# Self-attention in a decoder kernel: ScalarE copies the second bank of transposed probabilities in every step, VectorE the first bank only

## The reference, cut to what matters

```python
b, s, d = x.shape                      # s = 128 tokens in the kernel's view: (16, 128, 128)
xn = _rmsnorm(x, gamma1)
q, k, v = ...                          # 16 heads of 64
q, k = _rope(q, theta), _rope(k, theta)
scores = jnp.where(causal, jnp.einsum('bhqd,bhkd->bhqk', q, k) * scale, -jnp.inf)
attn = jax.nn.softmax(scores, axis=-1)
ctx = jnp.einsum('bhqk,bhkd->bhqd', attn, v)
attn_out = ctx @ o_w + o_b + xn
an = _rmsnorm(attn_out, gamma2)
aff = jax.nn.softmax(an @ router_w + router_b, axis=-1)
topv, topi = jax.lax.top_k(aff, K_ACT) # 3 of 31 experts per token
```

## Time and profile before

| | before |
|---|---|
| time, median of 3 executions | 1320.45 us (1319.38 to 1323.55) |
| the profiled execution: its own time | 1318.47 us |
| its span in the profile | 1316.7 us |
| PE busy | 1040.7 us, 79% of the span |
| DVE busy | 793.7 us, 60% |
| ACT busy | 579.6 us, 44% |
| POOL busy | 343.4 us, 26% |
| groups 0, 1, 2 of self-attention | from about 679 to 925 us, some 82 us each |
| group 3 with its `finish` pieces | from about 925 to 1059 us |
| experts | from about 1059 us to the end |

### The profile page before, as it was taken

The page is one execution under the profiler, slowest core; times in us unless marked ns, Lnnn a source line. Parts: engine busy times, 40 slices in busy tenths (PEclk is TensorE's granted clock), DMA queues, the critical chain, the costliest instruction groups (busy, mean ns, idle before and its releaser), DMA issues.

```text
span 1316.7 us, 20312 instructions
## 1 busy us (share of the span) xinstructions
PE 1040.7 (79%) x6091; PEld 660.4 (50%) x6121; DVE 793.7 (60%) x2206; ACT 579.6 (44%) x1439; POOL 343.4 (26%) x374
## 2 busy tenths in 40 slices
PE   5395575674768988988479989899876699999994
PEld 2242341331445665655136665666544566666662
DVE  6727638438455777676357667576665256666565
ACT  5345345345335777766124354343533133333331
POOL 3320320221351011111246456464742200000001
PEclk9597697786877999999579999999987689999997
DMA  5000000000000000000022212122110000000001
GB/s 170 2 17 6 2 16 6 2 16 0 0 12 29 13 25 14 1 1 1 14 60 56 65 38 58 40 56 64 33 41 1 1 13 16 20 16 19 17 16 37
DMA packets 43287, 33.37 MB, mean 25 GB/s; under 512 B 11266, under 2 KB 34018, under 8 KB 43234
## 3 DMA queue, kind: packets, MB, share of 16 engines
q1 hardware_dynamic: 43234, 32.70, 9.5%
HBM read 14.85 MB, written 1.05 MB: 12 GB/s over the span
## 4 chain that ended last, share of the span: by engine, by line
PE 61%; issue 18%; DVE 11%; POOL 6%; ACT 4%; SPq 0%; POOLq 0%; DMA 0%; DVEq 0%; ACTq 0%
PE psum L1675 10%; PE psum L1667 8%; PE psum L1542 5%; PE psum L1631 4%; PE psum L1595 4%; PE psum L1363 3%; PE psum L1370 3%; PE psum L1486 3%; PE psum L1611 3%; PE psum L1549 2%; PE psum L1556 2%; PE psum L1473 2%; PE psum L1467 2%; DVE negmax L1061 2%; POOL rT L568 2%
## 5 line engine op out<-in xcount | busy, mean ns | idle before, releaser
L1264 DVE SCALAR_TENSOR_TENSOR ntok<-psum,gate,ntok 128x128 f32<-128x128 f32 x512 | 144.3, 344 | 95.0 <-PE psum L1675 88.3
L1675 PEld LDWEIGHTS psum<-we,area 128*128 128x128 f32 x1024 | 129.2, 191 | 59.2 <-issue 30.8
L893 ACT ACTIVATE area<-psum,b1s 128x512 f32<-128x512 f32 x128 | 88.0, 687 | 150.3 <-PE psum L1667 147.7
L1675 PE MATMUL psum<-we,area 128*128 128x128 f32 x1024 | 137.9, 281 | 0.0
L865 ACT ACTIVATE area<-psum,negmax 128x128 f32<-128x128 f32 (+1 forms) x256 | 104.0, 423 | 69.1 <-DVE negmax L1165 69.1
L666 POOL TENSOR_TENSOR area<-area,rinv 128x512 f32<-128x512 f32 x64 | 94.3, 1474 | 140.3 <-DVE rinv L1221 140.3
L1667 PE MATMUL psum<-area,we 128*128 128x512 f32 x256 | 127.2, 600 | 0.0
L1128 DVE SCALAR_TENSOR_TENSOR area<-psum,ccol,cs 128x512 f32<-128x512 f32 x128 | 90.0, 745 | 52.4 <-PE psum L1542 51.0
L1542 PE MATMUL psum<-area,qkw 128*128 (+1 forms) x128 | 79.0, 702 | 35.4 <-DVE area L1134 18.4
L1061 DVE TENSOR_REDUCE negmax<-psum 128x2 f32<-128x512 f32 x128 | 82.3, 685 | 40.1 <-PE psum L1473 40.0
L797 ACT ACTIVATE area<-psum,negmax 128x256 f32<-128x256 f32 x256 | 102.0, 510 | 3.0 <-DVE negmax L1061 3.0
(11 more groups left out here) (215 smaller groups left out, 2002.2 us busy)
## 6 DMA issues: line engine op xcount, KB each, us to landing
area<-area SPq DMA_DIRECT2D x256, 64.0 KB, 2.0
we<-in_L_ffn_re_w SPq DMA_DIRECT2D x62, 64.0 KB, 1.8
area<-in_L_attn_W SPq DMA_DIRECT2D x8, 256.0 KB, 3.0
area<-in_mask_BxSxS_ik SPq DMA_DIRECT2D x8, 256.0 KB, 2.8
area<-in_x SPq DMA_DIRECT2D x4, 256.0 KB, 3.5
area<-in_ctx SPq DMA_DIRECT2D x8, 128.0 KB, 2.2
out<-ntok SPq DMA_DIRECT2D x4, 256.0 KB, 2.3
qkw<-in_L_ffn_q_w SPq DMA_DIRECT2D x1, 512.0 KB
```

The lines of the kernel that those rows point to most:

```text
L1264: last = nc.vector.scalar_tensor_tensor(res[:, n, :], bank[2 + g % 2][:, i * D:(i + 1) * D], gate[:, n, bass.ds(e, 1)], res[:, n, :], ALU. ...
L1675: last = nc.tensor.matmul(bank[2 + g % 2][:, i * D:(i + 1) * D], hE[:, g % 2, i * 128:(i + 1) * 128], we2[:, slot, :], start=True, stop=True)
```

## The change

In groups 0 to 3 the copy of bank 5 in the even steps goes from DVE to ACT. One constant changes; two places read it, which stay as they are.

```diff
         PARTS = ((0, 0, 1, 1), (0, 1, 0, 1))
-        ACT_COPIES = (1, 3)
+        ACT_COPIES = (0, 1, 2, 3)
         SU = 16
```

## The result

| | before | changed |
|---|---|---|
| time, median (6 runs each, taken together) | 1320.52 us (1318.38 to 1323.55) | 1328.37 us (1327.74 to 1329.41) |
| ratio, 95% interval | | 1.006 (1.0047 to 1.0073) |
| the profiled execution: time, span | 1318.47, 1316.7 us | 1327.88, 1326.1 us |

The forecast was 1322.2 us, the range ended at 1326.7. The kernel became slower by 7.9 us, outside both. First the page of the changed kernel: its span, its busy times, and the clock row of 40 slices.

The account below looks back on a forecast made before the run. PE was taken as nearly full in the loop (74.22 of 82.00 us). The terms 0 + 0.50 + 0.50 + 0.75 = +1.75 us on the median 1320.45 made 1322.2 us; the range was 1318.3 to 1326.7.

Parts of the forecast that it names:

- Bound and loop: Groups 0 to 2: PE nearly full, removed DVE time falls into its waits; 0, range -0.4 us per pass to nothing.
- Step 2 of the loop: Tightest place in groups 0 to 2: ACT's copy ends 1.76 us before PE's second half of turn(1) needs it.
- Step 4: Group 3: PE waits 0.46 us for ACT's copy; later POOL holds DVE's L1179 and L1187; +0.50 us.
- the bound without the lock: Group 3, step 4: cost if POOL did not hold DVE through shared SBUF ports, +0.05 us.
- Step 8: Group 3: ACT's queue 0.50 us later up to DVE's maxima; PE's scores delay caught in idle time; +0.50 us.
- Step 12: Group 3: ACT's copy delays turn(11), step 14's scores and logits by 1.0 us, 0.25 caught; +0.75 us.
- rival of the right kind and size: the clock: Group 3 around step 12: PE's rise to 2.4 GHz slips past step 15's maxima; +4.5 us more, 1326.7; chance 0.09.

Follow-up runs that it names:

- Run 8: Kernel before, with an ACT copy that nobody waits for behind the exponentials of steps 4, 8 and 12 of group 3: 1321.76 us, ratio 1.0012.
- run 7: Changed kernel with 14 useless transposes on PE in each of the waits inside turn(7) and turn(11) of group 3: 1323.07 us, ratio 1.0027.
- run 6: Kernel before, with only the even copy of step 10 of group 3 moved to ACT: 1325.34 us, ratio 1.0047.
- 2: Kernel before, with the even copies moved to ACT in group 3 only (8 copies): 1330.52 us, ratio 1.0075.
- run 10: Kernel before, with useless transposes at four of PE's old waits in group 3 (steps 10 and 14, turn(10), turn(14)): 1316.49 us, ratio 0.9965.
- 11: The useless transposes of run 10 put into the kernel of run 4: 1315.96 us, ratio 0.9961.
- 9: Kernel before, but in group 3 ACT copies every bank 5, odd steps too, one step after its scores: 1316.59 us against 1320.53, ratio 0.9971.
- 12: Kernel of run 9 with useless transposes on PE: 12 ahead of the wait in step 10, 5 in turn(10), 10 before step 14's gates: 1317.01 us, ratio 0.9976.
- 3: Changed kernel, but without moving the copies of steps 2, 6 and 10 of group 3 (29 of 32 move): 1321.06 us, ratio 1.0006.
- 4: Changed kernel with all 32 even copies on ACT, each one step earlier in ACT's order: 1319.56 us, ratio 0.9999.
- run 5: Kernel before, with only the even copy of step 6 of group 3 moved to ACT: 1322.98 us against 1319.86, ratio 1.0023.

## Why the prediction was wrong, point by point

**Bound and loop: right.** Step 2 of the loop was to stay covered with 1.76 us to spare, and no pass changed: 82.06 us from one L1556 to the next in both kernels, and no idle time of L1611 in the loop that ended with L874. Run 1 moves the 24 copies of the loop by themselves, for a ratio of 0.9998. DVE lost 2.1 us of busy time in a pass and nobody waited for it.

**Step 4: right.** PE's second half of `turn(3)` came at 946.59, which is 945.96 without the 0.63 us from the start; 945.93 was forecast. The mechanism held too: POOL's L647 (949.81 + 1.27) ends at 951.08 and DVE's L1179 (950.57 + 0.65) at 951.22, again 0.14 later. `gates` was 0.51 late, where +0.50 was forecast and +0.05 was the bound without the lock. In this kernel PE alone would have made L1179 late too: it starts 0.55 later than before, behind logits (L1564) that PE's wait held up. Run 8 has no such wait and tells the two apart. There the same operation (L1182) starts when it did before (952.35, which is 27.79 after L1556 in both), takes 1.21 us and not 0.70, and ends at 953.56, 0.14 after POOL (952.15 + 1.27 = 953.42); `gates` is again 0.50 late. The Trainium skill's port rule ("SBUF — State Buffer", section "SBUF: two separate sides") is again in agreement with these rows.

**Step 8: the failed step.** ACT's part was right: the second half of `turn(7)` started at 978.72, 0.26 earlier than 978.35 + 0.63. The prediction said that the wait "delays the scores by some 1.0, but that is caught in the 1.18 of idle time", and took +0.50. It priced all PE work behind the wait at 2.4 GHz. This work took 8.8 us from 978.72 to the end of the scores at 987.52; in run 7, at the upper level but for the first four transposes, 5.2 us (979.05 to 984.25). The difference is 3.6 us, and the term measured is +3.61. The idle time did catch what it was meant to catch. Before, PE idled for 0.61 + 0.42 + 1.18 = 2.21 us between the halves of `turn(7)` and the end of these scores, in the changed kernel not at all, and that pays for most of the 2.62 us by which the second half starts later (56.49 after L1556, before 975.03 + 0.44 - 921.60 = 53.87). The slower clock found nothing left to hide in. In run 7 the second half is 0.99 later still, and `gates` of step 10 is 1.23 late and not 3.84.

**Step 12: the same failure.** +0.75 was forecast, +4.90 measured in the changed kernel, +4.89 in run 6 alone (`gates` at 100.65), of which 3.95 are left by the experts. Here the prediction did have a rival of the right kind and size: the clock, already low ahead of `turn(11)`, rises only behind the scores of step 15, +4.5. It rose at 1021.4, behind these scores (1018.66 + 2.08). The rival had a chance of 0.09. It was looked for only where PE already ran slowly before, and not in step 8, where PE had been at 2.4 GHz throughout. With the rival in both places the sum would have been 1322.2 + 4.5 + about 3.5 = 1330, within 2 us of what was measured. The upper end, 1326.7, counted one place.

**Not in the prediction: the expert stage.** It took 1.3 to 1.6 us more in the changed kernel and in runs 2, 6, 7 and 8, 1.1 more in 10 and 11 and 0.4 to 0.5 in 9 and 12; in 1, 3, 4 and 5 it stayed within 0.3 of before. It is the clock at the beginning of the stage: granted 0.54 from 1067 to 1073 in the changed kernel, 0.69 from 1058 to 1064 before, and the first eight matmuls of L1675 take 1.91 us at 1070.60, before 1.05 at 1062.14. PE idles for 6.1 us ahead of the last `gates`, some 3.7 us before the stage. Which shift decides it is open: run 5 was 3.48 us late at the experts and kept its clock, run 8 was 0.50 late and lost it.

**What the runs show and what they don't.** Shown: three copies out of 32 carry the loss (3), two of them have their own each (5, 6), placed a step earlier they have none (4), and filling PE's wait removes all but 0.51 us of it ahead of the experts (7). Of the fourteen traces, the scores of step 10 take 1.23 us in just the three with the unfilled wait ahead of them (changed, 2, 5) and 0.71 or 0.72 in the others. Those of step 14 take 1.23 in the three with theirs (changed, 2, 6), but 1.12 to 1.23 in 10, 11 and 12 as well, which have no such wait. Shown too: the loss is the time for which the clock stays low, and a PE kept at work had it back within 4 us (7), where it had stayed low for 10 and 13. Not shown: what makes the clock fall or rise. The wait of 1.18 us in step 9 of before passes at the full clock, and so does that of 0.32 in step 4 of the changed kernel. The clock falls in the wait of 2.23, but in run 7 it falls in step 8 with that wait filled, in runs 8 and 12 it falls with no wait over 0.8 in the 5 us before, and ahead of those of 1.81 and 2.53 it was low already. No run varies the length of one wait by itself. The Trainium skill's "TensorE: Matmul & The Clock Gate", section "HAM oscillation — how this bites in real kernels", names waits between short bursts of matmuls as what throttles PE. By that rule the two places were suspects, and the rows agree in direction, though its waits are for DMA and longer than the 1.81 and 2.23 us here.

## What to carry to other kernels

A new wait on a TensorE that is full should have, as a rival with a real chance, the price of all the work behind it at half speed until the next point that someone waits for (here 9 us of work, 3.6 to 4.9 us of loss for a producer that was half a microsecond late). It is worth searching the trace of before for a stretch like that, since it shows the price, and for places where the clock is low already, since a new wait can keep it low. When a copy goes to another engine, its place in that engine's queue can matter more than whose time it uses: the same 32 copies on ScalarE cost 0.6% behind the exponentials of step `v + 2` and nothing a step earlier. Where PE has such waits anyway, useless transposes in them can pay (0.35% here), but each has to be measured, as the clock may then fall elsewhere.

## What was not expected of the hardware

- The 1.2 GHz stretch outlasted the wait by far: 2.23 us of idle time were followed by some 9 us of uninterrupted work at a granted clock of 0.57, and 1.81 us by 9.3 us at 0.53. PE at full load didn't bring the clock back at once. In run 7, where the useless transposes kept PE at work as the clock fell, it was back before the next scores.
- Doing more work on PE made the kernel faster: 57 more transposes in run 10, 1320.53 to 1316.49 us.
- A shift of half a microsecond, without any new wait, moved low-clock stretches about: run 8 lost 2.16 us by step 10, and had 0.50 at the experts.
